# Attention and expert layer on one core: score chunks in two pieces with other TensorE work between them

## What is computed

```
xn = layernorm(x)
q, k, v = Wq xn + bq, Wk ctx + bk, Wv ctx + bv
8 heads of 16 channels; position t attends to keys t-8 .. t+7 (zeros outside)
x1 = x + Wo softmax(q.k * 16^-0.5).v + bo
out = x1 + sum over the top 2 of 8 experts: weight * (layernorm(x1) A_e^T B_e^T)
```

## Time and profile before

| | |
|---|---|
| median of 3 runs | 1058.51 us (1055.99 to 1061.23) |
| profiled execution, its own time | 1057.9 us |
| its span, first to last instruction | 1056.1 us |
| PE, PE weight loads | 1011.5 us (96%), 869.8 us (82%) |
| DVE | 872.8 us (83%) |
| ACT | 582.5 us (55%) |
| POOL | 432.5 us (41%) |
| granted TensorE clock, mean | 0.987 |

### The profile page before, as it was taken

One profiled execution on the slowest core, in us unless ns is written; L12 is line 12 of the kernel. 1 busy time (PEld: TensorE's weight loads), 2 busy tenths in 40 slices (PEclk: granted clock), 3 DMA queues, 4 the chain that ended last, 5 costly groups with the idle time before them and its releaser, 6 DMA issues.

```text
span 1056.1 us, 54652 instructions
## 1 busy us (share of the span) xinstructions
PE 1011.5 (96%) x24508; PEld 869.8 (82%) x24508; DVE 872.8 (83%) x1889; ACT 582.5 (55%) x812; POOL 432.5 (41%) x373
## 2 busy tenths in 40 slices
PE   6879999999999999999999999999999999999987
PEld 5768888888888888888888888888888888888866
DVE  3778888888888888888889888889888888888852
ACT  6666555556555556555555555556555555654420
POOL 7773434434434434343434343444343443443210
PEclk9899999999999999999999999999999999999998
DMA  7232333322333322223332223332233332222210
GB/s 271 78 80 86 83 84 103 103 66 81 82 83 103 103 81 71 76 84 103 103 85 71 84 83 91 103 103 58 87 84 83 103 103 73 76 81 64 64 41 40
DMA packets 157721, 92.47 MB, mean 88 GB/s; under 512 B 139728, under 2 KB 139856, under 8 KB 157520
## 3 DMA queue, kind: packets, MB, share of 16 engines
q1 hardware_dynamic: 157520, 89.25, 28.9%
HBM read 55.16 MB, written 16.78 MB: 68 GB/s over the span
## 4 chain that ended last, share of the span: by engine, by line
PE 87%; issue 5%; DVE 5%; ACT 2%; DMA 1%; POOL 1%; DVEq 0%; SPq 0%
PE bank_a L351 35%; PE bank_b L401 18%; PE bank_c L351 16%; PE bank_b L380 13%; PE bank_a L410 5%; DVE stats L815 1%; DMA raw<-x 1%; DMA prob_t<-ctx 0%; DVE h_sb L875 0%; DVE row_max L886 0%; DVE row_sum L900 0%; DVE pick L861 0%; DVE resid_pair L954 0%; POOL x_split L1120 0%; ACT x_split L688 0%
## 5 line engine op out<-in xcount | busy, mean ns | idle before, releaser
L401 PEld LDWEIGHTS bank_b<-prob_t,v_diag 64*64 64x64 f32 x4608 | 192.0, 134 | 50.3 <-issue 41.9
L401 PE MATMUL bank_b<-prob_t,v_diag 64*64 64x96 f32 (+2 forms) x4608 | 211.4, 239 | 12.6 <-issue 12.2
L351 PE MATMUL bank_a<-down_split,mid_split 128*128 128x264 f32 (+1 forms) x1536 | 213.7, 289 | 1.5 <-DVE mid_split L934 1.4
L351 PEld LDWEIGHTS bank_a<-down_split,mid_split 128*128 128x128 f32 x1536 | 193.4, 188 | 8.6 <-DVE mid_split L934 2.3
L1091 POOL TENSOR_TENSOR prob<-prob,row_inv 128x512 f32<-128x512 f32 x128 | 134.2, 1049 | 159.0 <-DVE row_inv L904 157.2
L351 PE MATMUL bank_a<-up_split,ht_split 128*128 128x512 f32 x768 | 196.6, 407 | 2.8 <-DVE ht_split L941 2.8
L380 PEld LDWEIGHTS bank_b<-k_sb,q_diag 32*32 32x32 f32 x16384 | 155.0, 105 | 43.9 <-issue 36.7
L380 PE MATMUL bank_b<-k_sb,q_diag 32*32 32x32 f32 x16384 | 170.6, 195 | 10.7 <-issue 6.7
L351 PEld LDWEIGHTS bank_a<-up_split,ht_split 128*128 128x128 f32 x768 | 142.8, 192 | 33.7 <-DVE ht_split L941 3.3
L1114 POOL TENSOR_TENSOR attn_split<-attn,attn_split 128x1024 fp32r<-128x1024 f32 x32 | 76.1, 2378 | 145.6 <-ACT attn_split L676 145.6
L913 DVE STREAM_TRANSPOSE prob_t<-prob 128x768 f32<-128x768 f32 x128 | 122.9, 961 | 0.9 <-POOL prob L1091 0.9
(11 more groups left out here) (79 smaller groups left out, 1316.2 us busy)
## 6 DMA issues: line engine op xcount, KB each, us to landing
v_diag<-v_t SPq DMA_DIRECT2D x128, 132.0 KB, 3.3
raw<-x SPq DMA_DIRECT2D x32, 512.0 KB, 4.5
resid_pair<-x SPq DMA_DIRECT2D x32, 512.0 KB, 4.0
out<-resid_pair SPq DMA_DIRECT2D x32, 512.0 KB, 4.3
raw<-ctx SPq DMA_DIRECT2D x30, 512.0 KB, 3.3
stage<-down_w SPq DMA_DIRECT2D x2, 528.0 KB, 10.6
q_diag<-up_w SPq DMA_DIRECT2D x2, 512.0 KB, 5.7
prob_t<-up_w SPq DMA_DIRECT2D x2, 512.0 KB, 7.2
```

The lines of the kernel that those rows point to most:

```text
L351: return nc.tensor.matmul(dst, st[:, s, st_cols], mv[:, m, mv_cols], start=start and n == 0, stop=stop and n == 2)
L401: last = nc.tensor.matmul(bank_b[2 + m % 2][rows, lo * PW:hi * PW], value_blocks(b)[rows, n, :], prob_t[rows, at:at + (hi - lo) * KT], sta ...
```

## The change

`scores_chunk` is made of two calls of `scores_half`, each of 8 tiles: 32 calls, 64 matmuls with 64 weight loads. Only the second half tells `scores_done`. The head still gives whole chunks. In the steps Q stands between the halves of S1, the first part of D1 between those of S2, K between those of S3, and the first half of U1 between those of S0. The waits of `open_scores` stay in front of the first half.

```diff
             def scores_chunk(cur, m):
 
+                scores_half(cur, m, 0)
+                scores_half(cur, m, 1)
+
+            def scores_half(cur, m, half):
+
                 keys = k_sb[cur.parity]
-                for t in range(CT):
+                for t in range(half * CT // 2, (half + 1) * CT // 2):
...
-                last.then_inc(scores_done, 1)
+                if half == 1:
+                    last.then_inc(scores_done, 1)
...
                 if cur:
                     open_scores(cur, 1)
-                    scores_chunk(cur, 1)
+                    scores_half(cur, 1, 0)
...
                 if ahead:
                     project_q(ahead, (v_out, cur.count(1, 1)))
+                if cur:
+                    scores_half(cur, 1, 1)
...
                 if cur:
                     open_scores(cur, 2)
-                    scores_chunk(cur, 2)
+                    scores_half(cur, 2, 0)
...
                 for f in range(4):
                     down(1, f)
                 if cur:
+                    scores_half(cur, 2, 1)
+                if cur:
                     open_weighted(cur, 0)
                     weighted_chunk(cur, 0)
                 for f in range(4, FK):
                     down(1, f)
+                if cur:
+                    open_scores(cur, 3)
+                    scores_half(cur, 3, 0)
                 if ahead:
                     project_k(ahead, (q_out, ahead.count(2, 2)))
                 if cur:
-                    open_scores(cur, 3)
-                    scores_chunk(cur, 3)
+                    scores_half(cur, 3, 1)
...
                 if ahead:
                     pe.wait_ge(mask_set, ahead.count(CHUNKS, -1))
-                    scores_chunk(ahead, 0)
-                for e in range(EK):
+                    scores_half(ahead, 0, 0)
+                for e in range(EK // 2):
+                    up(1, e)
+                if ahead:
+                    scores_half(ahead, 0, 1)
+                for e in range(EK // 2, EK):
                     up(1, e)
```

## The result

The changed kernel takes 1086.2 us (median of 4, 1083.1 to 1088.8) against 1057.9 for the kernel before in the same comparison: ratio 1.026, 95% interval 1.022 to 1.030. It is slower, as forecast; 1079 was forecast and the range reached to 1090. The profiled execution took 1085.3 us, its span is 1083.5, against 1056.1. So 27.4 us have to be found.

What follows compares the result with a forecast made beforehand. TensorE's own row of work was taken as the bound. 1057.9 + 30.3 (shape changes) - 6.5 - 3.3 (shorter pauses) = 1078.4, forecast as 1079 us since the median shown is 0.6 above the profiled execution; range 1066 to 1090.

Steps and rivals of the forecast that it cites:

- What bounds: TensorE, busy 96% of the span, sets the end; every nanosecond between two of its matmuls counts in full.
- Round trip, 0.31 us: TensorE going to 32x32 scores and back costs 0.31 us; score chunk 2 adds only 0.11; +30.3 us in all.
- The other engines: VectorE's later score maxima just fit behind TensorE's work; mask and Q-evacuation waits stay hidden; cost 0.
- Pauses at S1, -6.5: Instruction-fetch pauses in score chunk 1 go, with 1.5 us more work ahead of the border; -6.5 us.
- Pauses at W0, -3.3: Fetch pauses in the first weighted chunk each shrink by 0.11 us over 30 steps; -3.3 us.
- DVE's margin: TensorE has 3.04 us of work while VectorE needs 2.99 before the down projection's first half continues; cost 0.
- The pauses at W0: Rival: the first weighted chunk's pauses go too, worth 18.5 us, 3.3 already in the sum; 1064 us; chance 0.12.
- Nothing is won: Rival: the pauses are not the instruction fetch's, or move to another place; 1089 us; chance 0.08.
- Faster: Rival: shorter score pieces leave TensorE's queue filled, shape changes cost 8 us against 25 of pauses; 1041 us; chance 0.04.

Runs made afterwards that it cites:

- S1-only kernel: Kernel before with only score chunk 1 given in two halves, the Q projection between them; 1057.4 us against 1057.6, ratio 0.999.
- shifted kernel: Kernel before with 36 tiny 32x32 products (144 instructions) ahead of the warm-up, steps unchanged; 1045.5 us, ratio 0.988.
- S3-only kernel: Kernel before with only score chunk 3 given in two halves, the K projection between them; 1069.2 us, ratio 1.012.
- pieces of 32: Changed kernel with score chunk 0 in four pieces of 32 matmuls, three up-projection matmuls after each; 1121.7 us, ratio 1.061 to the kernel before.
- S0-only kernel: Kernel before with only score chunk 0 given in two halves, half of the up projection's second half between; 1076.6 us, ratio 1.018.

## Why the prediction was right, and where its sum was off

- **What bounds.** Right: every term was found in PE's row, and a shift of the borders alone moved the time by 13 us.
- **Round trip, 0.31 us.** Mis-sized a little: 0.33 to 0.40, and 0.16 in place of 0.11 for S2. Two halves take 2 x 0.68 = 1.36 us against 1.21 + 0.115, since 64 matmuls take 0.75 - 0.195 = 0.555 us from the first start to the last, and 63 gaps of 8.6 ns would be 0.542. That explains 0.03 us a trip; the other 0.05 of S0's 0.40 is not explained. In the sum: 29 x (0.33 + 0.36 + 0.40) + 30 x 0.16 = 36.4 us, taken from one step each, where 30.3 was forecast.
- **O.** The step that failed is "The other engines": it looked at who waits for the masks and for Q's evacuation, and not at who waits for K's. S3's first half went ahead of K, which left 0.69 us of scores and 0.42 of transposes between K's end and O, for an evacuation that takes 1.11 and starts 0.11 late. 29 x 0.26 = 7.5 us, about the whole of the 7 us between forecast and result.
- **Pauses at S1, -6.5.** Right in size: S1, Q and D0's first part grew by 2.8 us over the 29 steps where the round trips alone are 9.3 (29 x 0.32, from 4.58 against 4.26 in steps without a pause), so 6.5 went. They also went in the S1-only kernel. But some of it is not a fetch pause (S1 takes 1.34 us to Q in every second step of the shifted kernel too, which has none), and the S3-only kernel has none of these pauses either.
- **Pauses at W0, -3.3.** In the view of waits they fell from 10.5 us over 19 to 4.9 over 12; in starts, all steps taken, from 19.3 to 13.4, so -5.9. The way was right, the size 2.6 us short, and kernels with the same order of PE differ by more (14.6 to 19.3), so the profile of one execution could not give this term better than to 5 us.
- **Together.** 36.4 + 7.5 - 6.5 - 5.9 = 31.5; the waits for h_sb (1.0 us in four steps, left out of the earlier trace rows) are gone too. The 29 full steps grew by 29.4 us in the traces and the spans by 27.4, so some 2 us were won in the head and the tail, where no term stood. All steps, means in us, from the starts of the groups:

| part | before | after | 29 steps |
|---|---|---|---|
| S1, Q, D0 first part | 4.527 | 4.625 | +2.8 |
| S2, D1 first part | 2.826 | 2.983 | +4.6 |
| W0 | 2.172 | 1.970 | -5.9 |
| D1 second part, K, S3 | 4.274 | 4.578 | +8.8 |
| transposes of h_sb, to O | 0.412 | 0.677 | +7.7 |
| S0, U1 | 4.069 | 4.463 | +11.4 |
| the whole step | 31.487 | 32.500 | +29.4 |

So the forecast of 1079 was low by one term at nothing (O) and by round trips 6 us too cheap, and part of that was hidden by what the pauses and the ends of the kernel gave.
- **DVE's margin.** The forecast of 3.04 us against 2.99 held: DVE's maxima of S1 start 1.43 us idle, and the low part that D0 waits for ends at 502.38, with D0's second part at 502.54, no wait.

```profile
499.50 0.69 DVE L902 TENSOR_REDUCE row_max<-bank_b 128x16 f32<-128x512 f32 x1 [1.43 <-PE bank_b L385]
...
501.73 0.65 DVE L950 TENSOR_TENSOR mid_split<-bank_a,mid_split 128x512 fp32r<-128x512 f32 x1
```

- **Rivals.** The pauses at W0 stayed in part. "Nothing is won" fell. The Trainium skill (Runtime: NRT & Kernel Launch, Instruction fetch mechanics) says that the cost of crossing a 16 KiB border is mostly hidden; in this kernel shifting the borders was worth 13 us. "Faster" fell with the halves (0.32 to 0.40 a trip) and with the pieces of 32, whose further trips cost 0.27. The Trainium skill (TensorEngine Tiling (Array Packing), Key Properties) says that a change of tiling mode drains TensorE; by that alone the prediction put the term at 20 us, and the rows gave 36.

## What to carry to other kernels

Where PE is the bound, count the changes of matmul shape: each way out and back cost 0.27 to 0.40 us here, as much as the pause that it was there to hide (S1) or more. If PE pauses at the same place of every step with no semaphore to blame, count whether the instructions from pause to pause are a multiple of 256 (here 508 of the trace from S1's to W0's, 512 with the 4 that do not show) before reordering the work: 144 tiny instructions ahead of the loop did what the splits did not. And when work is moved, list for each bank who writes it next, not only who reads it next: the wait that was missed was for the bank.

## What was not expected of the hardware

In this kernel a semaphore wait on PE's sequencer delays more than the matmul behind it. In the S0-only kernel `join_heads` ended 0.46 us before W2's first matmul and held none, yet PE's pauses in the next score chunk came to 9.9 us with it and to none with the same operation moved ahead on DVE, which gave back 12.4 us. By the count a border lies just behind that wait.

DVE's conversion of two indices (line 848, now 864) took 2120 ns on average in the kernel before and 253 ns in the changed one, which is most of DVE's 62 us less:

```profile
L864 DVE CAST top_atf<-top_at 128x2 f32<-128x2 uint32 x32 | 8.1, 253 | 1.1
```

In the kernel before it ran while GpSimd worked on the low part of the attention (2.4 us) and ended 0.02 to 0.03 us behind it, in all 30 such steps; in the changed kernel it runs ahead of it. In the S1-only kernel the order falls otherwise again: the conversion takes 322 ns, and DVE's `pick` (line 869) takes 621 ns on average in place of 288, its long ones ending 0.03 us behind GpSimd's product of the weights. So GpSimd held whichever of the two met it. No run was made to test this, nor what it cost PE.
